# Sorted rows in pieces of 128 with their own experts, taken in pairs, with W1 and bias loads placed ahead of them

## The reference, cut to what matters

```python
xn = layernorm(x)                                  # x: 16 x 256 tokens of 128
# attention: 16 heads of 8, keys and values shared by the heads
q = (xn @ w_q.T).reshape(B, S, 16, 8); k = xn @ w_k.T; v = xn @ w_v.T
s = softmax(einsum('bshd,btd->bhst', q, k) * scale) @ v  ...  @ w_out.T
# experts: rms norm, top 2 of 8 experts per token
t = xn * rsqrt(mean(xn * xn) + eps) * norm_scale
w = softmax over the two best of t @ gate_w + gate_b
y = sum over e of w[:, e] * (swiglu(t @ w1[e] + b1[e]) @ w2[e] + b2[e])   # w1: 128 x 512, w2: 256 x 128
out = x + s * silu(xn + y)
```

## Time and profile before

| | |
|---|---|
| median of 3 runs (lowest to highest) | 432.81 us (431.27 to 433.74) |
| the profiled execution's own time | 428.65 us |
| its span | 426.8 us |
| mean granted clock of TensorE, of full speed | 0.954 |
| busy: PE / PEld / DVE / ACT / POOL | 373.6 / 232.7 / 298.8 / 281.7 / 279.2 us |
| DMA traffic | 55.40 MB, 130 GB/s over the span |

### The profile page before, as it was taken

One profiled execution on the slowest core, in us unless ns is written; L12 is line 12 of the kernel. 1 busy time (PEld: TensorE's weight loads), 2 busy tenths in 40 slices (PEclk: granted clock), 3 DMA queues, 4 the chain that ended last, 5 costly groups with the idle time before them and its releaser, 6 DMA issues. The chain is left out here.

```text
span 426.8 us, 7861 instructions
## 1 busy us (share of the span) xinstructions
PE 373.6 (88%) x2375; PEld 232.7 (55%) x2375; DVE 298.8 (70%) x559; ACT 281.7 (66%) x617; POOL 279.2 (65%) x417
## 2 busy tenths in 40 slices
PE   1777789798989999999879997989989889998983
PEld 1665554233444444454459887978978754444321
DVE  6689758978997787777836664755665547888532
ACT  4963477566768787776836665655656468787992
POOL 6271053437888888888105887887688884387980
PEclk9988669799999999999969999999999999999997
DMA  6542227461232443312626766665665514535211
GB/s 169 137 130 75 90 87 242 179 243 50 72 97 68 139 132 99 104 67 76 180 60 170 197 179 192 182 193 162 187 180 161 145 44 146 151 102 149 66 43 45
DMA packets 51599, 55.40 MB, mean 130 GB/s; under 512 B 12036, under 2 KB 40580, under 8 KB 51431
## 3 DMA queue, kind: packets, MB, share of 16 engines
q1 hardware_dynamic: 46438, 45.45, 37.2%
q0 software_dynamic: 4544, 9.38, 6.4%
q10 hardware_dynamic: 576, 0.08, 0.1%
HBM read 34.46 MB, written 19.95 MB: 127 GB/s over the span
## 5 line engine op out<-in xcount | busy, mean ns | idle before, releaser
L1373 DVE TENSOR_REDUCE neg<-ps 128x4 f32<-128x1024 f32 x128 | 155.3, 1215 | 43.2 <-PE ps L932 37.4
L761 ACT ACTIVATE probs<-ps 128x512 f32<-128x512 f32 x256 | 141.9, 599 | 41.8 <-PE ps L917 33.8
L574 POOL DMA_INDIRECT y_dram<-early,xs x78 | 77.3, 991 | 47.5 <-ACT early L835 26.4
L917 PE MATMUL ps<-qs,k_stack 96*128 96x512 bf16 x256 | 91.1, 389 | 5.1 <-ACT probs L761 2.0
L932 PE MATMUL ps<-k_stack,qs 93*128 93x256 bf16 x512 | 82.0, 285 | 4.9 <-DVE neg L1373 4.8
L1083 PE MATMUL ps<-early,w_st 128*128 128x256 f32 x312 | 76.6, 389 | 9.9 <-DMA b_st<-b_col 4.6
L549 POOL DMA_INDIRECT sorted_dram<-rows,pos_i x64 | 65.0, 1016 | 11.2 <-POOL rows L544 9.9
L1449 DVE TENSOR_SCALAR early<-ps,b_st 128x256 f32<-128x256 f32 x78 | 34.2, 479 | 53.8 <-PE ps L1083 39.2
L945 PE MATMUL ps<-probs,v_all 128*32 128x512 f32 x512 | 69.3, 614 | 1.3 <-ACT probs L761 1.3
L1083 PEld LDWEIGHTS ps<-early,w_st 128*128 128x128 f32 x312 | 57.3, 194 | 19.0 <-issue 11.8
L932 PEld LDWEIGHTS ps<-k_stack,qs 93*128 93x128 bf16 x512 | 51.2, 102 | 26.3 <-issue 6.5
(11 more groups left out here) (156 smaller groups left out, 419.9 us busy)
## 6 DMA issues: line engine op xcount, KB each, us to landing
w_st<-in_w SPq DMA_DIRECT2D x39, 256.0 KB
qs<-q_dram SPq DMA_DIRECT2D x32, 288.0 KB
sorted_dram<-s_b SPq DMA_DIRECT2D x10, 520.0 KB, 4.3
xs<-sorted_dram SPq DMA_DIRECT2D x39, 130.0 KB
early<-y_dram SPq DMA_DIRECT2D x16, 256.0 KB, 4.2
q_dram<-early SPq DMA_DIRECT2D x16, 192.0 KB, 3.1
rows<-in_x SPq DMA_DIRECT2D x8, 256.0 KB
out<-rows SPq DMA_DIRECT2D x16, 128.0 KB, 2.0
```

The costliest lines, as they stand in the source:

```text
L574: gp.indirect_dma_start(out=y_dram, out_offset=bass.IndirectOffsetOnAxis(ap=at[:, t, :], axis=0), in_=ys[:, r, t, :], in_offset=None).then ...
L761: sc.activation(probs[:, u % 2, k, :], ps[:, bank, :], ACT.Exp).then_inc(m["exp_ok"], 1)
L917: te.matmul(ps[:, bank, :], k_stack[0:KALL, at:at + P], qs[0:KALL, u % QS, j * 512:(j + 1) * 512], start=True, stop=True).then_inc(m["exp_ ...
L1373: ve.tensor_reduce(neg[:, b % 2, st, h:h + 4], ps[:, 3 + 2 * (n % 2):5 + 2 * (n % 2), :].rearrange("p a (e t) -> p (a e) t", e=2), AX, ALU ...
```

## The change

The unit of sorting becomes a piece of 128 rows: PIECES = 64 + 7 = 71. An expert's rows begin at a piece. A step q takes a pair of pieces, 2q and 2q + 1 (the last step one), each with its own expert: 36 steps for 39. PE's first layer runs on 128 columns per weight in place of 256, the second layer reads an expert number and adds a bias per piece. ACT and DVE, whose biases now differ within a pair, run four instructions of 128 columns in place of two of 256.

W1 has eight slots in the buffer `early` (glu, lin and top move into a probability buffer), filled from w = 15 to 22, one a step. All 71 bias columns are copied from `b1_col` into one buffer by one DMA each, 18 per step in w = 16, 18, 20 and 17 in w = 22. The semaphore `b1_in` counts them, and ACT and DVE wait for all of them ahead of pair 0. `first_rows` stands ahead of the query load in w = 24. W1 of pair q + 3 is loaded in step q once the first layer of pair q - 1 is done.

values(20) moves from behind the experts to their steps q = -1 and 0. The first three matmul groups of w = 25 (`begin`) are issued at q = BLOCKS + 1 ahead of the last pair's second layer. The waits between both stages are spread over the ring's banks. Nine pad stores stand for ten. The bank numbers become functions of the pair.

```diff
-BLOCKS = TOPK * TOKENS // ROWS + E - 1
-WORDS = (BLOCKS + 7) // 8
+PIECES = TOPK * TOKENS // P + E - 1
+BLOCKS = (PIECES + 1) // 2
+WORDS = (PIECES + 7) // 8
-W_SLOTS, X_SLOTS, Y_SLOTS, HID = 3, 8, 4, 3
+W_SLOTS, X_SLOTS, Y_SLOTS, HID = 8, 8, 4, 3
+W1_AT, B1_AT = (15, 16, 17, 18, 19, 20, 21, 22), (16, 18, 20, 22)
+B1_STEP = -(-PIECES // len(B1_AT))
...
+def pieces(q):
+
+    return [(t, 2 * q + t) for t in range(2) if 2 * q + t < PIECES]
...
             def load_weights(q):
                 s = q % W_SLOTS
+                if q == 0:
+                    sp.wait_ge(m["route_ok"], 1)
+                    sp.wait_ge(m["qp_ok"], 4 * (len(CHUNKS) - 1))
+                    sp.wait_ge(m["kv_ps"], len(CHUNKS))
                 if q >= W_SLOTS:
-                    sp.wait_ge(m["h_ps"], 2 * (q - W_SLOTS) + 2)
-                    sp.wait_ge(m["glu_ok"], 2 * (q - W_SLOTS) + 2)
-                    sp.wait_ge(m["lin_ok"], 2 * (q - W_SLOTS) + 2)
+                    sp.wait_ge(m["h_ps"], 2 * ((q - W_SLOTS) // 2) + 2)
+                if q % 8 == 0:
+                    words.append(packed_experts(sp, q // 8))
                 e = expert_of(sp, words, q)
                 sp.dma_start(w1_st[:, s, :], w1[bass.ds(e, 1)].rearrange("a p c -> p (a c)")).then_inc(w_st[s], 16)
-                sp.dma_start(b1_st[:, s, :], b1_col[:, bass.ds(e, 1), :].rearrange("p a c -> p (a c)")).then_inc(w_st[s], 16)
+
+            def load_biases(h):
+                if h == 0:
+                    sp.wait_ge(m["b1_ok"], 2)
+                    sp.wait_ge(m["kst_sb"], len(KEY_BANKS))
+                    bias_words.extend(packed_experts(sp, i) for i in range(WORDS))
+                for q in range(h * B1_STEP, min((h + 1) * B1_STEP, PIECES)):
+                    e = expert_of(sp, bias_words, q)
+                    sp.dma_start(b1_st[:, q, :], b1_col[:, bass.ds(e, 1), :].rearrange("p a c -> p (a c)")
+                                 ).then_inc(m["b1_in"], 16)
...
-                i = q + W_SLOTS
-                if i < BLOCKS:
-                    if i + 1 < BLOCKS:
-                        load_sorted(i + 1)
-                    load_weights(i)
+                if q + 4 < BLOCKS:
+                    load_sorted(q + 4)
+                for t, i in pieces(q - 1 + W_SLOTS // 2):
+                    if i >= W_SLOTS:
+                        load_weights(i)
...
             def attend(u, w):
+                if w == EXPERTS_W - 1:
+                    first_rows()
                 if 1 <= u and u + 7 < UNITS:
                     load_q(u + 7)
...
-                if w == EXPERTS_W - 3:
-                    first_weights()
+                if w in W1_AT:
+                    load_weights(W1_AT.index(w))
+                if w in B1_AT:
+                    load_biases(B1_AT.index(w))
...
             def expert(q):
                 if q == -1:
-                    for i in range(BEFORE_EXPERTS - 3, BEFORE_EXPERTS):
+                    values(EXPERTS_AT - 1, 0)
+                    pe.wait_ge(*released(BEFORE_EXPERTS - 3))
+                elif q == 0:
+                    values(EXPERTS_AT - 1, 1)
+                    pe.wait_ge(m["max_ok"], 4 * EXPERTS_W)
...
+                elif q == BLOCKS + 1:
+                    begin(EXPERTS_AT, EXPERTS_W)
```

More of the change, by code:

```diff
@@ L416, in attend @@
                     for r in range(Y_SLOTS):
-                        sp.wait_ge(y_out[r], 32 * len(range(r, BLOCKS, Y_SLOTS)))
+                        sp.wait_ge(y_out[r], 16 * sum(len(pieces(q)) for q in range(r, BLOCKS, Y_SLOTS)))
                 for i in range(B):
@@ L570, in _ @@
                 pool.wait_ge(xs_in[q % X_SLOTS], 16 * (q // X_SLOTS) + 16)
[L571 removed]
+                pool.wait_ge(m["y_ok"], min(2 * q + 2, PIECES))
                 at = xs[:, q % X_SLOTS, :, D:D + 1].bitcast(I32)
[L573 removed]
+                for t, i in pieces(q):
                     gp.indirect_dma_start(out=y_dram, out_offset=bass.IndirectOffsetOnAxis(ap=at[:, t, :], axis=0),
@@ L757, in exps @@
                     act.wait_ge(m["pv_ok"], u - 1)
+                if first == 0 and u == EXPERTS_AT:
+                    act.wait_ge(m["hid_ok"], BLOCKS)
                 for k in range(first, end):
@@ L813, in expert @@
                     for c in range(2):
-                        sc.activation(glu[:, q % 2, c * ROWS:(c + 1) * ROWS], ps[:, 3 + 2 * (q % 2), c * ROWS:(c + 1) * ROWS],
-                                      ACT.Silu, bias=b1_st[:, s, c:c + 1], scale=ALPHA).then_inc(m["glu_ok"], 1)
-                if q == -1:
-                    sc.activation(root1[:, :], ones_f[:, 0:1], ACT.Silu)
+                        for t, i in pieces(q):
+                            at = slice(c * ROWS + t * P, c * ROWS + (t + 1) * P)
+                            last = sc.activation(glu[:, q % 2, at], ps[:, h_bank(q), at], ACT.Silu, bias=b1_st[:, i, c:c + 1],
+                                                 scale=ALPHA)
+                        last.then_inc(m["glu_ok"], 1)
                 if q == BLOCKS:
@@ L1082, in expert @@
                         for c in range(2):
-                            last = te.matmul(ps[:, 3 + 2 * r + h, c * ROWS:(c + 1) * ROWS],
-                                             w1_st[:, s, (2 * h + c) * P:(2 * h + c + 1) * P], xT[:, r, :],
-                                             start=True, stop=True)
+                            for t, i in pieces(q):
+                                last = te.matmul(ps[:, h_bank(q) + h, c * ROWS + t * P:c * ROWS + (t + 1) * P],
+                                                 w1_st[:, i % W_SLOTS, (2 * h + c) * P:(2 * h + c + 1) * P],
+                                                 xT[:, r, t * P:(t + 1) * P], start=True, stop=True)
                         last.then_inc(m["h_ps"], 1)
@@ L1090, in expert @@
                         pe.wait_ge(m["xsT_sb"], q + 1)
-                    for t in range(2):
-                        last = te.transpose(ps[:, 0, t * P:(t + 1) * P], xs[:, (q + 1) % X_SLOTS, t, 0:D], ident[:, :])
+                    for t, i in pieces(q + 1):
+                        last = te.transpose(ps[:, X_BANK, t * P:(t + 1) * P], xs[:, (q + 1) % X_SLOTS, t, 0:D], ident[:, :])
                     last.then_inc(m["xsT_ps"], 1)
```

140 lines of the change are left out of this document (77 added, 63 removed).

## The result

The changed kernel takes 449.55 us (median of 4 runs, 446.55 to 451.69); the kernel before, on the same chip, 432.04 (4 runs, 427.28 to 433.74). The ratio is 1.044, with a 95% interval of 1.032 to 1.055: **slower**. The forecast was 442.6 us, 7 too low.

What follows compares the result with a forecast made beforehand. GpSimd and TensorE were taken to pace the experts together, with SyncE's issues making them late. 426.8 + 23.0 - 9.8 - 2.0 - 1.4 = 436.6 us of span; +9.8 on the median gave 442.6 us, range 431 to 456.

Steps and rivals of the forecast that it cites:

- The start: Ahead of the experts: bias and W1 issues on SyncE delay the experts' first transpose to 237.3 us, +23.0 us.
- One bias load alone: 0.50 + 0.30 = 0.80: SyncE's queue, w = 16 to 22: issue plus register operations cost 0.80 us per bias load, 56.8 us for 71.
- rival A: SyncE's bias issues are cheap, 0.50 to 0.54 us each with register work overlapped; 424 us, faster; chance 0.15.
- The walk: SyncE's issues summed in order from w = 16: first rows asked for at 234.35 us, 25.3 us later.
- TensorE's waits ahead of w = 20, 22 and 24: Attention before the experts: TensorE stalls by some 7, 5 and 5 us, inside the 25 us and not added.
- this clock: Slow TensorE clock that may follow the stalls before the experts; not added, as SyncE stays later by 8 us.
- Three loops at 3.1, none with room: I keep the 3.25 us of before as pace.: Experts' stage: TensorE, GpSimd and ScalarE each need about 3.1 us per pair; pace kept at 3.25 us.
- rival B: Experts' stage: W1 traffic sets the pace at 3.5 us per pair, 8 us more; 451 us; chance 0.10.
- Three steps fewer: Experts' stage: 36 pairs in place of 39 blocks at 3.25 us save 9.8 us.
- The ends: Attention work moved at the experts' start and end: values(20) -2.0 us and begin -1.4 us.
- values(20) in idle time, -2.0: Its 16 matmuls move into TensorE's idle time ahead of the experts, saving 2.0 us behind them.
- begin, -1.4: First scores of w = 25, issued ahead of the last pair's second layer, fill idle time there, saving 1.4 us.

Runs made afterwards that it cites:

- e1: The changed kernel with its 71 bias loads at fixed columns and without the nine word reads, so without their register work; 434.1 us.
- e3: The changed kernel with W1 of pair q + 3 loaded ahead of the rows of pair q + 4 in SyncE's step; 439.7 us (two runs).
- e12: The changed kernel, bias loads and load order kept, with values(20) and begin back at their old places; 444.35 us, ratio 1.043 to the kernel before.
- e8: The kernel before with 71 bias loads into an unused buffer, five word reads, and ScalarE's wait for them ahead of block 0; 453.6 us (one run).
- e9: e6 with both values(20) and begin back at their old places; 413.55 us (4 runs).
- e11: e6 with begin back at its old place, only values(20) moved; 411.77 us (4 runs), ratio 0.969 to the kernel before.
- e10: e6 with values(20) back at its old place, only begin moved; 416.39 us (4 runs).
- e2: The changed kernel with nine loads of eight experts' bias columns in place of the 71 bias loads; 418.8 us.
- e4: The changed kernel with one W1 load per pair behind the first eight, in the old order; 442.4 us (one run).
- e6: e5 with W1 loaded ahead of the rows in SyncE's step; 418.86 us (4 runs), ratio 0.977 to the kernel before.
- e5: The changed kernel with the 71 bias loads replaced by five VectorE instructions that select the biases from columns on the chip; 421.0 us.

## Why the prediction was right in direction and 7 us low

The span measured and the span forecast differ by 444.8 - 436.6 = 8.2 us: 2.9 at the start, 0.3 in the first steps, 4.5 in the pace and 0.5 at the ends.

**The start, right in mechanism, 2.9 us low.** "One bias load alone: 0.50 + 0.30 = 0.80" measured 0.79, and in the same two parts. But the parts can't be taken away singly: the 0.30 of register work is worth 0.12 (e1), because an issue in a burst takes 0.60 where one with register work ahead takes 0.49. That is why rival A failed on its price and not on its reason: register operations do run beside the issue, but in no kernel here did a load get below 0.67 us in the mean, and A needed 0.50 to 0.54. The Trainium skill's rule ("DMA: Bandwidth & Descriptors", section "Issuing engines are not separate DMA queues") that initiating a DMA is usually small relative to the DMA fits the 256 KB loads (0.34 us of issue, 3.3 us to landing in e3). It is no guide to the 2 KB ones: whatever their transfers take, their issues held a queue for 56 us.

The walk came out 2.3 us short (first rows at 236.65, forecast 234.35). The bursts as a whole did not lose it: two ran at 0.75 and 0.74 a load, two at 0.86 and 0.81, in sum 0.5 us less than forecast. It is in the stretches between them, 5.2, 4.5 and 4.5 us where 3.9 was forecast. The landing took 3.5 us where 3 was estimated. TensorE's waits ahead of w = 20, 22 and 24 came as said but shorter, 3.7, 3.0 and 2.5 us where 7, 5 and 5 were forecast. Exponent scores of w = 20 and w = 24 still began 8.9 and 21.2 us late; part of that passed at the slow clock (granted 0.50 from 187 to 193 and from 207 to 213 us). The prediction named this clock and didn't add it, since SyncE stayed the later one, and that was right.

**The pace, the step that failed.** "Three loops at 3.1, none with room: I keep the 3.25 us of before as pace." The quiet step was forecast well, 3.10 for TensorE and 3.12 measured. But 3.25 was taken over as a total, without asking what makes up the 0.13 over the loops' 3.12. In the changed kernel it is a fourth loop, through SyncE: scatter, landing, row load, W1 load. The kernel before has it too: its first layers waited 4.6 us for the loads of a weight slot, three times:

```profile
PE ps L1083 <- DMA b_st<-b_col: 4.6, 3, 2.2
```

The prediction named that loop in rival B, priced it by traffic and gave it 3.5 us. The pace was 3.39, between both, and e3 shows that the order of two statements is enough to remove it, at more traffic, not less. The step is thus 0.14 x 32 = 4.5 us too cheap in this trace. Three steps fewer gave -5.3 in place of -9.8. How much of the 4.5 belongs to every execution stays open: e12, with the same loop, runs at 3.26, and e8, with the experts of the kernel before, at 3.18 where that kernel has 3.25. Where 3.25 came near, it was by luck, as nothing in the working led to it.

**The ends, right in size for a wrong reason.** -3.4 was forecast, -2.9 came. But e12, with neither move, is also 2.0 us shorter behind the experts than the kernel before (84.8 and 86.8 us). A likely reason is that the last step now has a single piece, which the prediction didn't price. From the last first-layer group to the scores pass 6.3 us in the kernel before (340.07 to 346.39) and 4.0 in e12:

```profile
357.85 1.06 PE L1132 MATMUL ps<-early 128*128 128x128 f32 x8
...
361.84 0.38 PE L961 MATMUL ps<-qs,k_stack 96*128 96x512 bf16 x1
```

The moves give a further 0.9 behind in the changed kernel, in one trace each. "values(20) in idle time, -2.0" can hold there, since TensorE waits for the rows anyway (14.0 us ahead of the first transpose with it, 14.3 without); e9 and e11 show -1.7 behind and +1.8 ahead once it doesn't wait. "begin, -1.4" is +2.1 in e10: the term counted 0.76 us of idle time that it would fill, and not the wait that it brings ahead of the second layer.

## What to carry to other kernels

Count the DMAs that a change puts into an in-order queue and price each by its issue in a burst, however few bytes it moves. If a small table is on the chip already, select from it with vector instructions. In such a queue put first what is ready first: a load with a free slot that stands behind a wait for another loop's landing inherits that loop's delays. And before work is moved into an idle gap, ask whether the gap survives the rest of the change, and what the moved work itself waits for.

## What the runs showed of the hardware

- A 2 KB load on SyncE takes 0.60 us of issue right behind another (0.67 from one to the next in the mean, e1), and 0.49 behind register operations (0.79 in all, the changed kernel; 0.71 in e8, where half of the loads have them). The register work is in part hidden, the issue is not.
- A bank wait and a gap of 1.07 and 0.50 us within 2 us were followed by a stretch at half clock in e1, e2, e4 and e6 (granted clock down to 0.50, 1 to 3 us longer behind the experts). The same gaps in the changed kernel, e3, e5 and e10 were not. What decides it stays open.
- DMA engines at a share of 0.88 and 265 GB/s didn't slow a loop whose loads are issued three steps ahead (e3).
